# A graph network on one core: the tiles that SyncE fetched go to GpSimd, and SyncE only lays the edge table

## What is computed

```
def rel_graph_conv(h, src, dst, etype, coef, bases, loopw, bias):
    hs = h[src]                                  # the gather of this study
    c = coef[etype]
    m = sum(c[:, b:b+1] * (hs @ bases[b]) for b in range(4))
    return segment_sum(m, dst) + h @ loopw + bias
...
x = _layernorm(x + L0(x))    # three relational layers: h = relu(conv(h)) + h
x = _layernorm(x + L1(x))    # mean of x[src] * weight per dst, then a linear map
x = _layernorm(x + L2(x))    # two relational layers: W[etype] @ x[src], summed per dst
x = _layernorm(x + L3(x))    # mean of x[src] per dst, then a linear map
```

## Time and profile before

| | |
|---|---|
| median of three runs | 8138.38 us (8128.93 to 8143.78) |
| the profiled execution's own time | 8131.88 us |
| its span, first to last instruction | 8129.8 us |
| busy, share of the span | PE 63%, PEld 53%, DVE 48%, ACT 19%, POOL 48% |
| granted TensorE clock, mean | 0.779 of full speed |
| DMA packets, and those under 512 B | 719134, 316147 |

### The profile page before, as it was taken

The page is one execution under the profiler, slowest core; times in us unless marked ns, Lnnn a source line. Parts: engine busy times, 40 slices in busy tenths (PEclk is TensorE's granted clock), DMA queues, the critical chain, the costliest instruction groups (busy, mean ns, idle before and its releaser), DMA issues.

```text
span 8129.8 us, 129078 instructions
## 1 busy us (share of the span) xinstructions
PE 5087.7 (63%) x26408; PEld 4271.0 (53%) x26409; DVE 3928.2 (48%) x10763; ACT 1515.1 (19%) x3108; POOL 3884.6 (48%) x4125
## 2 busy tenths in 40 slices
PE   4444444676666666666669985555555555555699
PEld 3444443666665666666655544444444444444455
DVE  3222222555555555555556654444444444444666
ACT  1111011222222222222220012222222222222101
POOL 5566554555555555555540005555555555555200
PEclk7777667777778777777779997777777777777799
DMA  2122122333333333333348863333333333333364
GB/s 76 48 53 55 51 53 58 97 107 104 100 99 104 96 100 104 96 96 100 98 119 286 282 199 71 73 75 76 72 76 71 72 70 71 69 69 69 109 182 153
DMA packets 719134, 804.75 MB, mean 99 GB/s; under 512 B 316147, under 2 KB 607471, under 8 KB 718543
## 3 DMA queue, kind: packets, MB, share of 16 engines
q0 software_dynamic: 131872, 271.19, 15.7%
q10 hardware_dynamic: 481717, 270.72, 11.2%
q1 hardware_dynamic: 105210, 259.53, 10.0%
HBM read 529.44 MB, written 277.57 MB: 99 GB/s over the span
## 4 chain that ended last, share of the span: by engine, by line
issue 25%; SPq 22%; PE 17%; another core or an unknown queue 14%; DVE 10%; DVEq 7%; ACT 2%; DMA 1%; ACTq 1%; POOL 0%; POOLq 0%
SPq L506 19%; PE sum L1033 6%; DVE acc L1366 3%; DVE bulk L1451 3%; SPq L502 3%; PE mixed L1132 2%; PE mixed L1033 2%; PE fill L1033 2%; DVEq L1451 2%; DVEq L1355 1%; DVE bulk L1447 1%; PE agg L1002 1%; DVE rel_w L1447 1%; ACT bulk L789 1%
## 5 line engine op out<-in xcount | busy, mean ns | idle before, releaser
L688 POOL DMA_INDIRECT bulk<-h_table,srcT_i x3276 | 3095.1, 945 | 3115.0 <-issue 891.7
L1366 DVE TENSOR_TENSOR acc<-mixed,acc 128x16 f32 x4160 | 729.3, 175 | 3283.0 <-remote 1978.2
L1132 PE MATMUL mixed<-bulk,mix_w 128*128 128x128 f32 x4992 | 1077.2, 392 | 908.1 <-ACT bulk L819 733.7
L1132 PEld LDWEIGHTS mixed<-bulk,mix_w 128*128 128x128 f32 x4992 | 1011.2, 297 | 1000.8 <-issue 855.0
L1122 PE MATMUL sum<-bulk 128*128 128x128 f32 x8320 | 1233.4, 297 | 313.4 <-DMA bulk<-lent 198.1
L1122 PEld LDWEIGHTS sum<-bulk 128*128 128x128 f32 x8320 | 1167.1, 214 | 334.5 <-DMA bulk<-lent 203.3
L1132 PE MATMUL mixed<-bulk,rel_w 128*128 128x128 f32 x3328 | 792.4, 415 | 494.7 <-ACT bulk L819 382.5
L688 POOL DMA_INDIRECT bulk<-in_x_dram,srcT_i x819 | 775.0, 946 | 564.2 <-issue 245.3
L1132 PEld LDWEIGHTS mixed<-bulk,rel_w 128*128 128x128 f32 x3328 | 712.7, 316 | 556.9 <-issue 377.7
L819 ACT ACTIVATE bulk<-sum 128x512 f32<-128x512 f32 x1040 | 619.9, 599 | 1764.9 <-remote 904.5
L1002 PE MATMUL fill<-bulk 128*128 128x196 f32 (+1 forms) x1664 | 398.6, 352 | 839.5 <-ACT bulk L789 758.4
(11 more groups left out here) (235 smaller groups left out, 3668.1 us busy)
## 6 DMA issues: line engine op xcount, KB each, us to landing
adjacency_w<-bulk ACTq DMA_DIRECT2D x416, 392.0 KB
bulk<-adjacency_w SPq DMA_DIRECT2D x147, 896.0 KB, 4.7
lent<-h_table SPq DMA_DIRECT2D x6656, 0.5 KB
adjacency_n<-bulk ACTq DMA_DIRECT2D x416, 196.0 KB
bulk<-adjacency_n SPq DMA_DIRECT2D x147, 448.0 KB, 3.9
bulk<-h_table,srcT_i POOLq DMA_INDIRECT x3276
lent<-in_x_dram SPq DMA_DIRECT2D x1664, 0.5 KB
bulk<-adjacency_w SPq DMA_DIRECT2D x49, 448.0 KB, 4.2
```

What stands on the lines that cost most here:

```text
L688: nc.gpsimd.indirect_dma_start(out=rows_in[:, s, :], out_offset=None, in_=rows_of[:, :], in_offset=bass.IndirectOffsetOnAxis(ap=srcT_i[:, ...
L1132: last = nc.tensor.matmul(MSG[h][:, 0:HALF * WIN], W[:, n, :], sums[:, h, n, :, :].rearrange("p t v -> p (t v)"), start=(n == 0), stop=(n ...
L1366: nc.vector.tensor_tensor(acc[:, at], MSG[h][:, s * WIN:(s + 1) * WIN], acc[:, at], ALU.add).then_inc(added[s], 1)
```

## The change

The lent tile goes. GpSimd's loop loses its `continue` and gathers all 16 slots in every turn; TensorE waits for `gathered[s]` alone; `fetch`, `place` and `lend_passes` go, with `lent`, `lend_at`, their four semaphores, the DMA that loads `lend_at` and VectorE's multiply of it. What stays of SyncE's work in the relational layers is `lay_table` in the first: before part n it waits for the `summed[3]` for which `place(n)` waited too. The eight `added` semaphores stay as they are.

```
-            def lend_passes(l):
-                    for n in range(QUADS):
-                        fetch(l, n, sp.snap(K + n))
-                        place(n, sp.snap(K + n))
-                        if laying:
-                            table_part(n)
+            def lay_table():
+
                 more = sp.value_load(passes[0:1, 1:2], min_val=0, max_val=MAX_PASSES - 1)
+                for n in range(QUADS):
+                    sp.wait_ge(summed[3], sp.snap(more * TURNS + (n * QUAD + QUAD)))
+                    apart(sp)
+                    table_part(n)
...
             for l, layer in enumerate(LAYERS):
                 if layer["kind"] == REL:
-                    lend_passes(l)
+                    if l == 0:
+                        lay_table()
                     continue
...
                             for s in range(HALF * h, HALF * (h + 1)):
-                                if s == RING - 1 and i % QUAD == QUAD - 1:
-                                    continue
                                 nc.gpsimd.indirect_dma_start(
...
                                 for t in range(4):
-                                    if 4 * q + t < RING - 1:
-                                        pe.wait_ge(gathered[4 * q + t], landed)
-                                    else:
-                                        pe.wait_ge(gathered[4 * q + t], gathers_there)
-                                        pe.wait_ge(lent_placed, lent_there)
+                                    pe.wait_ge(gathered[4 * q + t], landed)
...
-            dve.wait_ge(lent_in, 16)
-            nc.vector.tensor_scalar(lend_at[:, :], lend_at[:, :], float(ROW_BYTES), None, ALU.mult).then_inc(lend_set, 1)
```

More of the change, by code:

```diff
@@ L28 @@
 BF16 = mybir.dt.bfloat16
-U8 = mybir.dt.uint8
 I32 = mybir.dt.int32
@@ L34 @@
 DVE = mybir.EngineType.DVE
-SP = mybir.EngineType.SP
 D = 128
@@ L57 @@
 LAG = 4
-LOADED = 32
-ROW_BYTES = 4 * D
 SHORT_LAG = 2
@@ L309, in build @@
         share = sb("share", [D, BLOCKS_OF])
-        lent = sb("lent", [D, 2, D])
-        lend_at = sb("lend_at", [1, QUADS * D], I32)
         ident = sb("ident", [128, 128])
@@ L393, in build @@
         gathered = [sem(f"gathered{s}") for s in range(RING)]
-        lend_set = sem("lend_set")
-        lent_in, lent_landed, lent_placed = sem("lent_in"), sem("lent_landed"), sem("lent_placed")
         onehot_ready = [sem(f"onehot_ready{q}") for q in range(4)]
@@ L450, in build @@
         rows_from = [x] + [tables[(l - 1) % 2] for l in range(1, len(LAYERS))]
-        def gathers(s):
-            return GATHER_PASS - 16 * QUADS if s == RING - 1 else GATHER_PASS
         def apart(eng):
@@ L485, in _ @@
             sp.dma_start(srcT_i[:, :], src_cols).then_inc(src_in, 16)
-            sp.dma_start(lend_at[:, :].rearrange("o (n e) -> o n e", e=D),
-                         src[0:TILES * D].rearrange("(n o e) -> o n e", o=QUAD * RING, e=D)[QUAD * RING - 1:QUAD * RING, :, :]).then_inc(lent_in, 16)
             sp.dma_start(type_i, etype.rearrange(block_of, p=BLOCK, e=D)).then_inc(type_in, 16)
@@ L493, in _ @@
             P = sp.value_load(passes[0:1, 0:1], min_val=1, max_val=MAX_PASSES)
[L495 to L515, removed]
             def reaching(flat, first, end):
@@ L533, in table_part @@
                     sp.dma_start(edge_rows[first:end, 2 * D:3 * D], reaching(weight_flat, first, end)).then_inc(edges_out, 16)
-            def lend_passes(l):
-                if l:
-                    for j in range(2):
-                        sp.wait_ge(rows_dma[j], 16 * dma_before(l, j) + 16)
-                else:
-                    sp.wait_ge(lend_set, 1)
-                def lend_pass(p, laying):
-                    K = sp.snap(P * (REL_BEFORE[l] * QUADS) + p * QUADS)
-                    for n in range(QUADS):
-                        fetch(l, n, sp.snap(K + n))
-                        place(n, sp.snap(K + n))
-                        if laying:
-                            table_part(n)
[L550 to L553, removed]
+            def lay_table():
                 more = sp.value_load(passes[0:1, 1:2], min_val=0, max_val=MAX_PASSES - 1)
[L555 to L558, removed]
+                for n in range(QUADS):
+                    sp.wait_ge(summed[3], sp.snap(more * TURNS + (n * QUAD + QUAD)))
+                    apart(sp)
+                    table_part(n)
             def load_adjacency(m, matrix, B, pass_of):
@@ L695, in _ @@
                         for h in range(2):
-                            pool.inc_swdge_sem(gathered[HALF * h:HALF * (h + 1)], [gathers(s) for s in range(HALF * h, HALF * (h + 1))],
+                            pool.inc_swdge_sem(gathered[HALF * h:HALF * (h + 1)], [GATHER_PASS] * HALF,
                                                mode="sub")
@@ L928, in _ @@
                 pe.sem_inc(summed[q], 1)
-            pe.sem_inc(lent_placed, 1)
             for h in range(2):
@@ L1105, in messages @@
                     def messages(i, k, between=None):
-                        gathers_there = pe.snap((i * 3 + 2) // QUAD * 16 + (gathers(RING - 1) * r + 16))
-                        lent_there = pe.snap((k + 1) // QUAD * 16 + 1)
                         this, following = pe.snap(k + 1), pe.snap(k + 2)
```

1 line of the change is left out of this document (removed).

## The result

After: 7892.84 us in the median of 4 runs (7886.32 to 7905.09). Before, on the same chip: 8141.08 (8128.93 to 8148.91). The ratio is 0.9701, 95% interval 0.9689 to 0.9712: 248 us less, where I had forecast 103 and a lower bound of 7975. The direction was right, the size was 2.4 times too small. (And on one chip, further down, even the direction was another.)

What follows compares the result with a forecast made beforehand. GpSimd's gathers were taken to set the pace, with TensorE stalling on SyncE's late lent tiles. 71 - 146 - 9 - 19 = -103 us gave about 8029, predicted as 8035 us against a median of 8138.38; range 7975 to 8108.

Steps and rivals of the forecast that it cites:

- No price for less traffic: The sum gave no credit for SyncE's 8320 row DMAs going away, leaving that to the rivals.
- The gap shrinks: Rival: without SyncE's small DMAs GpSimd's 2.9 us gap before halves falls, 52 us per 0.1; 7932 us at 0.2; 6%.
- the sign of being wrong that I had named: Wrong if GpSimd idles after TensorE's sums in other turns, or if the gap between halves moves at all.
- Stalls removed, -146: TensorE's waits before tile 15 for the lent tile, counted as far as they reach GpSimd: 146 us saved.
- the layer's end, -9: First layer's last turn: TensorE's 9.03 us wait for the lent tile goes, nothing of GpSimd's absorbing it.
- The bounds of 100 to 198: Stalls' credit: 198 us if every stall counts, 100 if the other engines' loop keeps a third.
- Gathers, +71: GpSimd's 65 added gathers at 1.25 us cost 81 us, less 10 hidden; bounds 71 to 81.
- The step that hid 10 of them: Third and fifth layers: the half's eighth gather disappears in GpSimd's waits for chunk steps and in last turns: 8 x 1.25.
- Table, -19: Edge table's last part goes out a turn earlier; second layer's first sums come after 51 us instead of 70.1.
- The range: 7975 to 8108 us, cut from bounds summed as -147 to -19, that is 7991 to 8119.
- The stalls come back: Rival: the other engines' loop is late each fourth turn by itself, stall credit vanishes: +43, 8181 us; 6%, within 0.2% 4%.
- half comes back: Rival: the loop's 1 us slack is used up, about 70 of the 146 stay: -33, 8105 us; 12%.

Runs made afterwards that it cites:

- c_after: The kernel after, unchanged, as third-group control beside the kernel before on the same chip: 7776.35 us, ratio 0.9756.
- e1_rows_all: The kernel after plus 128 single rows fetched by SyncE each fourth turn in all five relational layers, unread and not waited for: 7976.16 us, ratio 1.0003 to before.
- third and fourth group's chips: Where the kernels with row fetches beside in all five layers ran with unchanged controls; before took 7976 and 7966 us, after 0.9756 and 0.9758 of it.
- first group's: Chip where after with unread row fetches in four layers ran against register loads only, and before with cheaper lent fetches; before took 8103 us.
- e3_65_fewer: The kernel after with the sixteenth tile of each fourth turn gathered by nobody, 65 gathers fewer: 7686.46 us, ratio 0.9646 to before.
- the chip without gaps: Fifth group's chip, where GpSimd's gaps before halves are 0.30 us: before 6372.26 us, after 6451.68, ratio 1.0130.
- e4_late_part: The kernel after with the edge table's last part waiting one turn longer, for the layer's last sums: 7788.53 us, ratio 0.9768 to before.
- the last group: Fifth group: after unchanged and after with GpSimd waiting by quarters, against before at 6372.26 us: 6451.68 (1.0130) and 6450.47 (1.0125).
- c3_after: The kernel after, unchanged, as fifth-group control on the chip where before takes 6372.26 us: 6451.68 us, ratio 1.0130.
- e1_rows_beside: The kernel after plus 128 single rows fetched by SyncE each fourth turn in the second to fifth layers, unread: 8005.65 us, ratio 0.9891 to before.
- e1_loads_only: The kernel after with SyncE only loading those row numbers into registers, no DMA issued, second to fifth layers: 7870.11 us, ratio 0.9714 to before.
- e6_four_dmas: The kernel after plus 128 rows fetched beside per four turns, in four DMAs of 32 rows, in place of 128 DMAs: 7794.37 us, ratio 0.9788 to before.

## Why the prediction was wrong

*The step that failed* is "No price for less traffic", with the rival *The gap shrinks* that I gave 6%. The rival named the cause (SyncE's small DMAs) and its place (the 2.9 us before halves); its slope (52 us for each 0.1) held for half of the price only. From `c_after` to `e1_rows_all` the median gaps grow by 0.19 us on average, 99 us for the 515, and the gaps' sum by 218. Of the rest, 63 are in the waits after chunk steps (from 67 to 82 us over the median in the third layer, from 23 to 70 in the fifth). I argued it away with one row, 2.83 at 7601.19 while SyncE was idle, against "2.9 is usual". But a gap has to be set against its own layer: the median of the fifth was 2.96. In that layer of the trace of before five gaps have no SyncE fetch in the 13 us ahead of them, 2.72 to 2.86, and those beside a fetch have a median of 2.97; in the third three, 2.84 to 2.88, against 3.04. After gave 2.74 and 2.84. These are eight gaps, but they stood in the trace, and the row that I quoted against the rival spoke for it. Measured, the row DMAs are worth 200 and 205 us on the third and fourth group's chips, 136 in four layers on the first group's. That the gap moved at all was the sign of being wrong that I had named.

*Stalls removed, -146, and the layer's end, -9.* Too large. Nothing measures them alone; for the result's chip they follow from the rest: 248 = traffic + stalls + 17 (table) - 88 (gathers), so 319 less a traffic of 170 (136 x 5/4) to 205: 114 to 149 in place of 155, an estimate that takes prices from other chips. On the third group's chip 0 = 88 - stalls - table, with 10 to 19 for the table: 69 to 78, though there the idle time by my way of counting was only 62, so the count itself isn't what erred there. The bounds of 100 to 198 held for the result's chip, not for that one.

*Gathers, +71:* 88 by `e3_65_fewer`, 79 on the chip without gaps. The step that hid 10 of them in the third and fifth layers' chunk waits failed. With 65 gathers fewer the three waits of the third layer add up to 22.9 us over the median, with them to 23.4 (`e3_65_fewer`, `e4_late_part`), so nothing is hidden there; in the fifth it is 13.7 and 10.1, some 3.6 hidden. The waits also shrank as a whole (13.04 to 10.87).

*Table, -19:* the mechanism was right, VectorE second in line included. The first sums moved by 16.6 us in the result's profiles, and undoing it costs 10 to 19 in the timelines. GpSimd waits 14.92 us for the table where I had 10, since the last part went out 17.7 us before the end of the last sums and not 25.

*The range.* Its bounds were added up wrongly: 71 - 198 - 9 - 19 is -155 and 81 - 100 - 9 is -28, where I had -147 and -19. The right ones don't reach -248 either; what lies beyond them is the term that the sum didn't have.

*The stalls come back; half comes back.* Neither held for the result, but in the third and fourth groups the change without its traffic gave nothing, which lies between their -33 and +43; I had given them 18% together.

*What held:* The direction for the result's chip, 4160 gathers at 1.25 us, no wait for a lent tile, no new wait of SyncE that anything stands behind, GpSimd as the pacer: 65 gathers fewer are worth their full length. The Trainium skill's half sentence on faster DMAs from Sync (DMA: Bandwidth & Descriptors, "Issuing engine by pattern") doesn't hold for such gathers here, by more than I had it: on the chips with the gaps a tile costs SyncE some 96 us of queue and the turn 2 to 3 us in other engines' waits, where GpSimd needs 1.25.

## What to carry to other kernels

Many small DMAs from an engine that is off the path are not free: before you leave out the price of traffic, split the pacer's gaps by whether that traffic ran, within one layer, and compare medians and not one row with a round number. A stall that is the difference of two near periods is worth little as a forecast; where the fetch took 3 us less, the idle time behind it was 62 us and not 157. And where the trace names no cause for the pacer's gap ("remote"), the result may not hold on every chip: time both kernels on several.

## What the hardware showed

- **TensorE's sums reach the other engines late while GpSimd issues indirect DMAs**, in the profile of the result and those of four groups: a median of 3.5 to 4.2 us from the modelled end of a sum to ScalarE's start, and the signal itself mostly 1.9 us after a burst; in the last group, 0.04 and none. GpSimd's gap before a half is 2.4 to 3.1 us where this is so and 0.30 where it isn't. That it alone makes 7770 of what can be 6452 isn't shown; no run switched it off. The Trainium skill (Perfetto Trace Analysis, "Tensor Engine Instruction (MATMUL, LD_WEIGHTS)") says that TensorE's end is an estimate, and that the update follows only when PSUM has acknowledged the bytes. The traces don't tell which of the two is late, the write or its announcement; nor do the runs tell why the last group was free of it, and whether the chip or its condition made it so.
- **DMAs of one row from SyncE** cost the turns 16 to 30 ns each on the chips with the gaps (16 with fixed addresses, 25 with loaded ones, 30 with 64 a quad), and 64 bytes hardly less than 512. On the chip without them before must have had next to no stalls, since after is slower there by 79 us, nearly its 81 of gathers; with quads of 80 us (`c3_after`) its fetch can't have taken 96. There is room for it: in the trace of before the commonest step from one row DMA to the next is 0.32 us, 41 us for 128, and single steps of 0.7 and 1.4 us make up the rest of the 96. What these steps wait for, and whether they are gone on that chip, no trace shows.
- The Trainium skill (DMA: Bandwidth & Descriptors, "Why a DMA increments its semaphore by 16 and not by 1") says that for a DMA on fewer than 16 engines the issuing sequencer writes the missing increments itself. A row DMA would be such a case: SyncE's queue has 92522 packets in `e1_rows_beside` and 79210 in `e1_loads_only`, two for each of the 6656 DMAs, one of data and one of 4 bytes, where the 256 DMAs of `e6_four_dmas` have 48 each, 32 of them rows. No run here took the increments away and left the DMAs, so it is only a candidate for what their number costs.
- The same two programs gave 0.9701, 0.9756, 0.9758 and 1.0130 in four places.
